# A decoder layer on one core: the convolution of its last FFN moved between engines, one shared identity, and a reordered head of the mixing stage

## The reference, cut to what matters

```python
h = bit_linear(x, w1)                                   # 512 -> 2048, rounded x, ternary w
h = depthwise_conv1d(h.transpose(0, 2, 1), conv_w, conv_b)   # 3 taps over time
h = jax.nn.silu(h.transpose(0, 2, 1))
return bit_linear(h, w2)                                # 2048 -> 512, h rounded at 127 / max|h| of its token
```

## Time and profile before

| | |
|---|---|
| median of three runs | 3562.73 us |
| the profiled execution | 3561.91 us |
| its span | 3560.3 us |
| mean granted TensorE clock | 0.957 of full speed |
| busy: PE, PEld | 3177.0 (89%), 2286.5 (64%) |
| busy: DVE, ACT, POOL | 2358.0 (66%), 1769.2 (50%), 1127.6 (32%) |
| last FFN, its DMA issues to the end | about 3097 to 3560 us |

### The profile page before, as it was taken

One profiled execution on the slowest core, in us unless ns is written; L12 is line 12 of the kernel. 1 busy time (PEld: TensorE's weight loads), 2 busy tenths in 40 slices (PEclk: granted clock), 3 DMA queues, 4 the chain that ended last, 5 costly groups with the idle time before them and its releaser, 6 DMA issues. The chain is left out here.

```text
span 3560.3 us, 57155 instructions
## 1 busy us (share of the span) xinstructions
PE 3177.0 (89%) x19234; PEld 2286.5 (64%) x19234; DVE 2358.0 (66%) x4214; ACT 1769.2 (50%) x3131; POOL 1127.6 (32%) x892
## 2 busy tenths in 40 slices
PE   6998999999999999689996898599999999467887
PEld 5776666666666666467775777477887888334443
DVE  5562888888888888555553788634445444379996
ACT  3331888888888888412222222132222222066662
POOL 2343222311321231143331355311111111058886
PEclk9999999999999999889997999799999999689999
DMA  6775212211311222355644443321111110201112
GB/s 216 242 244 166 67 57 74 77 60 56 91 60 57 69 80 64 123 188 187 226 167 155 135 142 124 101 95 42 42 42 43 42 41 30 80 23 54 60 42 71
DMA packets 239608, 350.54 MB, mean 98 GB/s; under 512 B 31792, under 2 KB 129104, under 8 KB 239440
## 3 DMA queue, kind: packets, MB, share of 16 engines
q1 hardware_dynamic: 208784, 291.46, 25.3%
q0 software_dynamic: 8640, 31.77, 2.7%
q10 hardware_dynamic: 22016, 25.17, 2.0%
HBM read 210.68 MB, written 137.64 MB: 98 GB/s over the span
## 5 line engine op out<-in xcount | busy, mean ns | idle before, releaser
L863 DVE CUSTOM_DVE_ANT_0 attend_scores<-attend_scores,attend_bias_table 128x1024 f32<-128x1024 f32 x512 | 630.4, 1231 | 164.0 <-PE attend_scores L717 157.7
L790 ACT ACTIVATE attend_probs<-attend_scores,attend_neg_max 128x1024 f32<-128x1024 f32 x512 | 571.2, 1116 | 136.9 <-DVE attend_neg_max L863 126.8
L729 PE MATMUL attend_turned<-attend_ident,attend_probs 128*128 128x128 f32 x4096 | 557.5, 275 | 11.5 <-DVE attend_probsT L871 11.2
L729 PEld LDWEIGHTS attend_turned<-attend_ident,attend_probs 128*128 128x128 f32 x4096 | 473.0, 141 | 121.4 <-DVE attend_probsT L871 27.2
L717 PE MATMUL attend_scores<-attend_k_stack,attend_q_stack 96*128 96x512 f32 x1024 | 375.2, 448 | 14.4 <-DMA attend_q_stack<-qk_parts 9.8
L798 ACT COPY attend_probsT<-attend_turned 128x512 f32<-128x512 f32 x640 | 359.1, 583 | 25.4 <-PE attend_turned L729 23.5
L2207 DVE TENSOR_TENSOR cross_ffn_h_lo<-cross_ffn_hidden,cross_ffn_h_hi 128x512 fp32r<-128x512 f32 x128 | 96.3, 757 | 361.9 <-ACT cross_ffn_h_hi L2104 361.3
L691 POOL TENSOR_TENSOR attend_out_parts<-attend_out_full,attend_out_parts 128x256 fp32r<-128x256 f32 x64 | 46.5, 727 | 856.7 <-ACT attend_out_parts L805 856.7
L744 PE MATMUL attend_out_acc<-attend_probsT,attend_v_in 128*32 128x256 f32 x4096 | 312.9, 389 | 0.7 <-DVE attend_out_full L881 0.7
L871 DVE COPY attend_probsT<-attend_turned 128x512 f32<-128x512 f32 x384 | 263.4, 686 | 1.3 <-PE attend_turned L729 1.3
L717 PEld LDWEIGHTS attend_scores<-attend_k_stack,attend_q_stack 96*128 96x128 f32 x1024 | 154.1, 190 | 171.4 <-issue 169.2
(11 more groups left out here) (302 smaller groups left out, 6630.0 us busy)
## 6 DMA issues: line engine op xcount, KB each, us to landing
qk_parts<-qkv_qk_out SPq DMA_DIRECT2D x64, 512.0 KB, 3.2
attend_k_stack<-qk_parts SPq DMA_DIRECT2D x192, 128.0 KB, 2.5
attend_q_stack<-qk_parts SPq DMA_DIRECT2D x192, 128.0 KB, 2.6
qkv_wq_raw<-L_ffn_w POOLq DMA_DIRECT2D x16, 1024.0 KB, 7.8
o_parts<-attend_out_parts ACTq DMA_DIRECT2D x64, 256.0 KB, 2.5
mix_in_o_in<-o_parts SPq DMA_DIRECT2D x32, 512.0 KB, 6.7
qkv_x_in<-x SPq DMA_DIRECT2D x8, 1024.0 KB, 6.0
v_rows<-qkv_v_out SPq DMA_DIRECT2D x32, 256.0 KB, 3.4
```

The source lines that it names most:

```text
L729: last = pe.transpose(turned[:, x, c], probs[:, i % 2, k * P:(k + 1) * P], ident[:, :])
L790: act.activation(probs[:, i % 2], scores[:, i % 2], ACT.Exp, bias=neg_max[:, i % 4:i % 4 + 1], scale=-1.0, accum_out=den[:, qg % 2, j, h:h ...
L863: dve.tensor_tensor_reduce(scores[:, i % 2], scores[:, i % 2], bias_table[:, h, at:at + T], -1.0, BIG, ALU.add, ALU.min, neg_max[:, i % 4: ...
```

## The change

1. **Last FFN.** ScalarE no longer computes the right tap, and its tile is gone. VectorE's `add_left` writes its sum back into PSUM `centre` instead of `conv`, and a new `add_right` on VectorE, one instruction, adds y shifted the other way times the right weight, from PSUM to `conv`. GpSimd's `add_right` is gone; GpSimd does `round_block` for the first seven units instead, with its own order (scale, round). The last unit is still rounded by VectorE (`round_last`), under a new semaphore. VectorE's order in a step becomes dequantise, left tap, maximum, right tap. All lags behind the left tap are one step shorter. What waited for the right tap's activation now waits for `right_added`.
2. **One identity** for the whole kernel, built in the first stage; the other five stages no longer build and wait for their own.
3. **Head of the mixing stage.** Wout and its bias are loaded on GpSimd's queue at the start of `attend`, into tiles that live through both stages, and split by GpSimd in its first turn. At the end of `attend` SyncE loads x, waits for all stores, and loads the first `o_in`; GpSimd adds the bias. In `mix_in` the context comes first, then k and v, the second `o_in`, q. VectorE begins with `residual_norm(0)`, then k, `split_emb`, v, q. The waits for the small biases stand later.

```diff
-    SILU_AT, TURN_AT, MAX_AT = 3, 4, 5
-    SPREAD_AT, SCALE_AT, ROUND_AT = HB + 5, HB + 6, HB + 7
+    SILU_AT, TURN_AT, MAX_AT = 2, 3, 4
+    SPREAD_AT, SCALE_AT, ROUND_AT = HB + 4, HB + 5, HB + 6
...
-                def add_right(i):
-                    pool.wait_ge(right_ready, i + 1)
-                    pool.wait_ge(left_added, i + 1)
-                    pool.tensor_tensor(conv[:, i % CR], conv[:, i % CR], right_tap[:, i % 2], ALU.add).then_inc(right_added, 1)
...
+                def round_block(i):
+                    u, f = divmod(i, HB)
+                    pool.wait_ge(h_scaled_ready, i + 1)
+                    if f == 0:
+                        past(pool, out_ready, (u - 1) * HT)
+                    pool.tensor_scalar(hqT[:, u % 2, f], h_scaled[:, i % 2], ROUND, -ROUND, ALU.add, ALU.add).then_inc(hq_ready, 1)
...
-                    past(act, right_added, i - 1)
-                    act.wait_ge(y_edged, i + 1)
-                    act.activation(right_tap[:, i % 2], y[:, s, i % 2, 2:HALF + 2], ACT.Identity, scale=taps[:, f, 2:3])\
-                        .then_inc(right_ready, 1)
...
+                    dve.scalar_tensor_tensor(out=centre[:, i % 2], in0=y[:, u % 2, i % 2, 0:HALF], scalar=taps[:, f, 0:1], in1=centre[:, i % 2],
+                                             op0=ALU.mult, op1=ALU.add).then_inc(left_added, 1)
+
+                def add_right(i):
+                    u, f = divmod(i, HB)
+                    dve.wait_ge(left_added, i + 1)
                     past(dve, silu_done, i - CR + 1)
-                    dve.scalar_tensor_tensor(out=conv[:, i % CR], in0=y[:, u % 2, i % 2, 0:HALF], scalar=taps[:, f, 0:1], in1=centre[:, i % 2],
-                                             op0=ALU.mult, op1=ALU.add).then_inc(left_added, 1)
+                    dve.scalar_tensor_tensor(out=conv[:, i % CR], in0=y[:, u % 2, i % 2, 2:HALF + 2], scalar=taps[:, f, 2:3], in1=centre[:, i % 2],
+                                             op0=ALU.mult, op1=ALU.add).then_inc(right_added, 1)
...
                 for s in range(END):
-                    i = block_at(s, MAX_AT)
-                    if i is not None:
-                        find_max(i)
                     if s < SLOTS:
                         dequantise(s)
                     i = block_at(s, 1)
                     if i is not None:
                         add_left(i)
+                    i = block_at(s, MAX_AT)
+                    if i is not None:
+                        find_max(i)
+                    i = block_at(s, 1)
+                    if i is not None:
+                        add_right(i)
...
+                def load_first():
+
+                    sp.wait_ge(wout_step, 2)
+                    sp.dma_start(first["x_in"][:, :, :], half_of(x, 0)).then_inc(x_loaded, 16)
+                    sp.wait_ge(out_stored, KB * G * 16)
+                    for g in range(KB):
+                        sp.dma_start(first["o_in"][:, g].bitcast(F32), o_parts[0, g, :, :, 0:HALF]).then_inc(first_loaded, 16)
...
-                dve.wait_ge(biases_loaded, 5 * 16)
-                split_w(0, "out")
+                residual_norm(0)
                 split_w(1, "k")
-                residual_norm(0)
+                split_emb(0, 0)
                 split_w(2, "v")
-                split_emb(0, 0)
                 split_w(3, "q")
+                dve.wait_ge(biases_loaded, 4 * 16)
```

More of the change, by code:

```diff
@@ L42, with memory @@
 RSQRT_SEED = float(0x5F3759DF)
-def memory(nc, ctx, stage):
+def memory(nc, ctx, stage, own=True):
     def sb(name, shape, dt=F32):
@@ L58, in clear_semaphores @@
         nc.all_engine_barrier()
-    ctx.callback(clear_semaphores)
+    if own:
+        ctx.callback(clear_semaphores)
     def sem(name):
@@ L538, in _, with attend @@
                 pair(B - 1, True, False)
-def attend(nc, qk_parts, v_rows, o_parts):
+def attend(nc, ident, qk_parts, v_rows, o_parts, x, Wout, bout, first):
     GH = P // DH
@@ L692, in low_part, with split_wout @@
                         .then_inc(out_lo_ready, 1)
+                def split_wout():
+                    raw = first["x_in"][:, :, :]
+                    pool.wait_ge(wout_loaded, 32)
+                    pool.tensor_copy(first["w_hi"][:, :, :], raw).then_inc(wout_step, 1)
+                    pool.wait_ge(wout_step, 1)
+                    pool.tensor_tensor(first["w_lo"][:, :, :], raw, first["w_hi"][:, :, :].bitcast(F32), ALU.subtract).then_inc(wout_step, 1)
                 def body(turn):
                     tables(turn)
+                    if isinstance(turn, int) and turn == 0:
+                        split_wout()
                     for qg in range(G):
@@ L700, in _ @@
                 turns(pool, body)
+                pool.wait_ge(x_loaded, 16)
+                for t in range(HT):
+                    pool.tensor_tensor(first["x_in"][:, t], first["x_in"][:, t], first["bias"][:, :], ALU.add).then_inc(x_biased, 1)
                 low_part(TURNS, 0)
                 low_part(TURNS, 1)
+                pool.wait_ge(x_biased, HT)
             @block.tensor
             def _(pe):
-                pe.wait_ge(ident_step, 2)
                 def score(turn, i):
@@ L925, in mix_in @@
         NAMES = ("out", "k", "v", "q")
-        SOURCES = dict(out=Wout, k=wk, v=wv, q=wq)
-        w_hi = {m: sb(f"w{m}_hi", [P, KB, D], F32R) for m in NAMES}
-        w_lo = {m: sb(f"w{m}_lo", [P, KB, D], F32R) for m in NAMES}
-        bias_out = sb("bias_out", [P, D])
+        SOURCES = dict(k=wk, v=wv, q=wq)
+        w_hi = {m: sb(f"w{m}_hi", [P, KB, D], F32R) for m in NAMES[1:]}
+        w_lo = {m: sb(f"w{m}_lo", [P, KB, D], F32R) for m in NAMES[1:]}
+        w_hi["out"], w_lo["out"] = first_in["w_hi"], first_in["w_lo"]
+        o_in, x_in, bias_out = first_in["o_in"], first_in["x_in"], first_in["bias"]
         bias_o = sb("bias_o", [P, D])
@@ L1101, in _ @@
             def _(pool):
-                for tile, vector in ((bias_out, bout), (bias_o, bo), (bias_q, bq)):
+                for tile, vector in ((bias_o, bo), (bias_q, bq)):
                     pool.dma_start(tile[:, :], row(vector, 0, D)).then_inc(biases_loaded, 16)
@@ L1121, in embed @@
                         pool.tensor_tensor(emb[:, t], emb[:, t], ctx_in[:, t], ALU.add).then_inc(emb_ready, 1)
+                    if isinstance(n, int) and n == 0:
+                        pool.wait_ge(biases_loaded, 4 * 16)
                     for t in range(HT):
@@ L2379, in _ @@
                         scale_block(i)
-                    i = block_at(s, 1)
-                    if i is not None:
-                        add_right(i)
+                    i = block_at(s, ROUND_AT)
+                    if i is not None and i < LAST * HB:
+                        round_block(i)
             @block.tensor
```

124 lines of the change are left out of this document (56 added, 68 removed).

## The result

The changed kernel takes 3719.61 us (median of 4 runs, 3717.93 to 3724.64), beside 3562.35 for the kernel before (4 runs in the same set): ratio 1.0443, 95% interval 1.043 to 1.0456. The forecast was 3713.0, range 3668 to 3761. The profiled execution has a span of 3717.4 us against 3560.3, 157.1 more, and a mean granted clock of 0.943 against 0.957.

The account below looks back on a forecast made before the run. The prediction took VectorE and GpSimd, holding each other in the last FFN, as the bound, and expected a new 3.81 us loop. From 3561.91 us, FFN +161, mixing head -11 and start +1 gave 3713 us, range 3668 to 3761.

Parts of the forecast that it names:

- The loop and its length: Last FFN: maximum, transposes, next product, dequantisation, left tap and next maximum form a loop within one step, 3.81 us per block.
- Idle before line 2414's transposes released by block_max in nearly all steps: Last FFN: a sign that would show the forecast right, TensorE's transposes waiting for the maximum over the block before.
- The FFN's sum: Last 122 steps of the last FFN: steps, scales, spread, edges and clock total 523 us, against 361 before.
- clock's two terms: Last FFN: half-clock steps cost 12 us after stalls and 26 (two thirds of 39) in 31 steps before the w2 products.
- The scales: Last FFN, once in 16 blocks: the tiny instruction takes 0.20 beside idle GpSimd, so 1.63 us instead of 2.70; 2 in all.
- The rounding on GpSimd: Last FFN: a 128x512 rounding takes 0.8 us, bounded by 0.29 and 1.29, and costs nothing on the path.
- rival (a): Last FFN: the maximum does not gate the next step, VectorE's own work sets the pace; 3534 us, chance 0.07.
- The end: Last FFN, from the last dequantisation to the scales: 8.9 us instead of 12.2, -3.
- The head: Start of the mixing stage: earlier loads and residuals first gain 11 us (4 to 12); attention's start costs +1.
- (b): Last FFN: GpSimd's rounding takes over 2.5 us and GpSimd becomes the bound; 3810 us, chance 0.03.
- (c): Last FFN: the clock is at half throughout, the w2 part too; 3828 us, chance 0.04.
- (d): Last FFN: transposes do not wait as read, GpSimd's new pair is as slow as the old; within 0.2%, chance 0.02.

Follow-up runs that it names:

- filled kernel: The changed kernel with four more matmuls of 128x512 in each of the 36 steps before the second product, into an unread bank: 3682.61 us.
- old_ffn_band: old_ffn with SyncE loading the first position-bias band ahead of the first half's stores in the first mixing stage: 3543.68 us, ratio 0.9946 to the kernel before.
- old_ffn: The changed kernel with the last FFN of the kernel before put back, keeping only the one identity: 3552.78 us, ratio 0.9971 to the kernel before.

## Why the prediction came out as it did

**The loop and its length: right.** Forecast 0.82 + 0.47 + 1.27 + 0.60 + 0.65 = 3.81, measured 0.83 + 0.47 + 1.26 + 0.61 + 0.65 = 3.82. All five terms came from rows of the kernel before. That the right tap lies in the time between maximum and dequantisation is right as well. Taking the product or the maximum out of its place removes 125 or 128 us of the change's price of 157.

**"Idle before line 2414's transposes released by block_max in nearly all steps": wrong as a sign.** The profile named the silu in 125 steps. The silu of another block ended 0.11 us after the maximum, 0.03 before the transposes. The forecast should have asked which other engine's event falls at that moment. The experiments had to decide it, and they decided for the maximum.

**The FFN's sum: 523 forecast, 523.8 measured, by terms that partly make each other good, so that the nearness of the two is in part luck:**

| | forecast | measured |
|---|---|---|
| 122 steps | 464.8 | 466.0 (122 x 3.82) |
| scales and spread, 7 times | 2 + 8 | 8.0 (7 x (0.29 + 0.85)) |
| edges and single steps | 10 | 13.9 |
| clock | 12 + 26 = 38 | 0.2 + 35.7 = 35.9 |

The measured terms of the first three lines are from the gaps of the filled kernel (487.9 us in all), the last is 523.8 - 487.9. Of the 13.9 the edges are 12.4, 4.1 each where 3.48 had been counted. Of the clock's two terms the one for the steps before the second product was too small: from the sixth to the 38th dequantisation the changed kernel takes 35.7 us longer than the filled one, against 26. The half-clock step itself, 5.07, was right (5.12). The 12 for the time after stalls were too many: behind the 38th dequantisation the two kernels differ by 0.2. The two thirds of 39 were a choice between two rows, and nearer to 39, which the prediction set beside its 26, would have been right.

**The scales: right.** The tiny instruction took 0.17 us instead of 1.27, since GpSimd was idle beside it in the first seven units, and this is what the forecast's 1.63 rested on.

**The rounding on GpSimd: 0.8 taken, 0.29 to 1.29 as bounds, 1.93 measured.** The bound was wrong. I held that an operation with two inputs is above one with one input and two constants; the rows say that on GpSimd the operation with constants is dearer already with one of them (1.49 against 1.28), and 0.44 more with the second. It cost nothing in the step, as forecast, because 1.28 + 1.93 is below 3.82. But it spoils rival (a): had the loop not been there, the time would not have been 3534 but, as an estimate, about 3592, which is what the kernel with the maximum first took. Beside a pair of 2.1 us VectorE would have set the pace; a pair of 3.31 is longer than VectorE's mean step, 2.8 (three of 2.65 and one of 3.30).

**The start: +2 forecast, +3.1 measured. The end: -3 forecast, -0.9 measured.** The scales of the last unit start 8.8 us after the last dequantisation (3664.30 after 3655.49), as forecast (8.9, though the terms written down for it, 1.25 + 4 x 1.7 + 0.6, add up to 8.65). But GpSimd is in the middle of the last roundings when the scale row is there:

```profile
3667.65 0.59 ACT L2513 COPY quantised_ffn_scale_row<-quantised_ffn_spread 128x512 f32<-128x512 f32 x1 [6.98 <-PE quantised_ffn_spread L2432]
3667.84 1.94 POOL L2385 TENSOR_SCALAR quantised_ffn_hqT<-quantised_ffn_h_scaled 128x512 bf16<-128x512 f32 x1
3669.94 1.26 POOL L2378 TENSOR_TENSOR quantised_ffn_h_scaled<-quantised_ffn_h,quantised_ffn_scale_row 128x512 f32<-128x512 f32 x1
```

Its first scale starts 1.7 us after the row is written, and one more rounding (1.92 us, at 3671.17) stands behind it. I had weighed the work that was moved to GpSimd against the step, and not against its queue at the end, where GpSimd still has roundings to do when the last unit's scales come; before, it had none then.

**The head: -11 +1 forecast, -8.0 at the FFN's first dequantisation, -10.7 by the run without the FFN's change.** Two of its steps were wrong, in opposite directions. The first: "only the 2 MB of `o_in` follow the stores". The description of the change above, which has SyncE wait for all stores, is wrong in the same way: by the code (`out_stored` at KB * G * 16) the loads wait for the stores of the first batch alone, and they were issued at 1417.6, some 58 us before attention's last store; so the first product waited for no load and began at 1480.3, not 1486.6. The second: "TensorE is at 9 tenths in the slices behind, so little of it is lost". A gain of 15.8 us at the transposes met a load that had not been moved, and 7.6 of it were lost, 2 of these by the clock. Up to the end of attention the changed kernel is 2.5 us later (its last store is issued at 1476.01 instead of 1473.55) where +1 was forecast. Of this 0.6 is there already at the end of the first stage, which varies by up to 1.8 us between executions of the same code (341.79 in old_ffn_band, 343.63 in old_ffn). The two DMA issues ahead of the iota take 0.78 and 0.56, and the first exponential of attention starts at 358.81 instead of 355.36; no run separates the rest.

**The rivals.** (a) was ruled out by the pitch; (b), GpSimd as the bound, by the rounding back on VectorE, which left the step as it was; (c) by the 3.82 us of the steps in the later part, the length at full clock; (d) by the size of the effect.

## What to carry to other kernels

Where one buffer ties two engines together and one of them works in order, write down the loop from the consumer's instruction back to itself and count what each engine has between the two ends: here an instruction between dequantisation and maximum cost its whole length in each step (3.16, 3.82, 4.62 us), and one behind the maximum cost nothing in the ordinary step as long as VectorE's own work was shorter than the loop. One remedy needs no other buffer: issue work that needs nothing ahead of the instruction that waits. It took the loop away and not the whole loss, for the kernel was still 33 us slower than the one before. And when a stage's head is moved forward, look for the next load in the same queue that was not moved; it took half of the gain.

## What the runs showed of the hardware

Some VectorE instructions from SBUF to SBUF wait for the GpSimd instruction that is running: the `tensor_scalar` of 128x4 elements takes 0.17 us beside an idle GpSimd and 1.29 beside a product that started 0.02 us before it, and the two end together. A rounding of 128x512, also a `tensor_scalar`, takes 0.42 us beside an idle GpSimd, and 0.88 beside a product. In the kernel with the maximum first the tiny instruction ended together with GpSimd's running rounding in six of seven units, and in one it did not wait. It does not hold for every instruction between SBUF tiles: in the kernel before, the tiny reduction (line 2551) takes 0.20 us beside GpSimd's running addition, and 0.21 beside nothing. The taps and the maximum, which read PSUM, show none of this. The Trainium skill (SBUF — State Buffer, SBUF: two separate sides) calls the pair of ports that the two engines share an exclusive lock held for the whole instruction. The rows beside a product agree. Beside a rounding not all do: in six units of the kernel with the maximum first the `tensor_scalar` of line 2571 started 0.09 us behind GpSimd's rounding, took 0.54 us and ended 1.29 before it.

GpSimd's time on 128x512 of f32 went by the operation and not by the output's type (bf16 or f32): copy 0.61, one constant 1.49, two 1.93, product of two inputs 1.28 us.

TensorE's clock can fall in a steady loop: with 2.3 us idle before the transposes of each step it was 0.55 over 100 us, and four more matmuls per step brought it to 0.98, which made the kernel 37 us faster. With the maximum in fourth place, which left TensorE up to 2.26 us idle before the transposes instead of 1.47, it was 0.79 in a part where it had been 0.97.
